# Row maxima of attention scores: reductions of up to 1024 columns over two PSUM banks, in a ring of two pairs, with one bank for the outputs

## The chip, the core and the metric

One Trainium2 chip, one of its cores. The metric is the device time of one execution in microseconds (us), as the median of several runs. TensorE (PE in the profile) multiplies, VectorE (DVE) and ScalarE (ACT) work on what it leaves in PSUM, GpSimd (POOL) does small work in SBUF, and SyncE (SP) issues most of the DMAs. PSUM has eight banks of 512 float32 values per partition. A matmul here writes into one bank at a time.

## The reference, cut to what matters

Two layers of a hybrid model run over 2048 tokens of width 128: a Mamba block, a mixture of experts, attention, experts again, a second Mamba block, a quantised MLP, attention with ALiBi, and the MLP again. The change touches the two attentions. Each has 16 heads of width 8, and is causal:

```python
dots = jnp.einsum('bhid,bhjd->bhij', q, k) * scale
causal = jnp.triu(jnp.ones((n, n), dtype=bool), k=1)
dots = jnp.where(causal, mask_value, dots)
attn = jax.nn.softmax(dots.astype(jnp.float32), axis=-1).astype(dots.dtype)
out = jnp.einsum('bhij,bhjd->bhid', attn, v)
```

The softmax subtracts each query's largest score before it exponentiates. That maximum is what the changed code finds.

## The kernel before

The 2048 tokens are NT = 16 tiles of 128 and NC = 4 chunks of 512. For each head, `attention` computes the scores twice.

The first time it does so with queries on the partitions, to find the maxima. An *item* is one query tile t against one key chunk kc, up to 512 keys wide; `q_items` lists the 40 items of a head, numbered 0 to 39 here. Tiles 0 to 3 have one item each (0 to 3), tiles 4 to 7 two each (4,5 to 10,11), tiles 8 to 11 three each (12,13,14 to 21,22,23) and tiles 12 to 15 four each (24..27 to 36..39). A tile's last item is 128, 256, 384 or 512 columns wide, in turn, and the others 512. PE makes an item with four matmuls of 32 weight columns each (L1679), which run side by side; DVE then takes its maximum, with `tensor_reduce` (L1861), or with `tensor_tensor_reduce` (L1858, CUSTOM_DVE in the profile, followed by a READ_ACCUMULATOR) where the item holds the diagonal and the causal mask must be added. After item 39, L1866 folds a tile's maxima together, GpSimd splits them into three bfloat16 parts (L1942 to L1947), PE transposes these (`turn`, L1663), DVE copies them out (L1849, CAST), and SP writes them by DMA into the operand `q_op` as three more rows (L2030).

The second time the scores come with keys on the partitions, the maxima already subtracted by those three rows. A *score* is a key tile against a query chunk (L1693, with a causal mask on the diagonal ones, L1697), 40 per head. ACT exponentiates it (L1797), and PE multiplies four at a time with v (`times_v`, L1715, float32, in two instructions each). When a query chunk is done, ACT copies the outputs from PSUM (L1805) and SP stores them.

PE's order is written out by hand: score b+3 of the running head, then the item at position 54+b of the item stream, and after every fourth b a `times_v`. So the items run one head and 14 positions ahead of the scores, and score 0 of a head comes right after item 10 of the next one. `times_v` stands behind items 1, 5, 9, 13 and so on; those behind items 13, 25 and 37 are diagonal ones with narrower pieces. The transposition `turn` of a head stands ahead of item TURN = 5 of the next. The first 54 items run before any score. Waits are in order on each engine.

PSUM: three banks `ps_k` for scores (KB = 3), three banks `ps_q` for items, transpositions and the later `direct` and `output` products (QB = 3), and two banks `ps_o` for the outputs. Each use of `ps_q` has a number, and `bank_free(use)` (L1650) lets PE write use u only when DVE has read use u-3. `times_v` waits at the start of a chunk only for the copy of the chunk before last (L1707), since two banks alternate.

```python
            def bank_free(use):
                if use >= QB:
                    pe.wait_ge(q_read, use - QB + 1)
```

Of the kernel before, what the change touches and what calls it, by code (L numbers as in the profile page):

```python
# [21 lines left out]
ALU = mybir.AluOpType  # L22
# [4 lines left out]
P = 128  # L27
# [1453 lines left out]
def attention(nc, g, w, tag, dram, x, xn, alibi):  # L1481
# [4 lines left out]
    with ExitStack() as ctx:  # L1486
# [6 lines left out]
        QB = 3  # L1493
        LEAD = 14
        TURN = 5
# [33 lines left out]
        maxes = m.sb("maxes", [P, NT, NC])  # L1529
# [58 lines left out]
        NQ = len(q_items)  # L1588
        q_begins = [min(i for i, (t, kc) in enumerate(q_items) if t // TPC == c) for c in range(NC)]
# [16 lines left out]
        item_use, turn_use = {}, {}  # L1606
        for p in range(POSITIONS):
            if turned_at(p) is not None:
                turn_use[turned_at(p)] = len(item_use) + len(turn_use)
            if p < NQ * HEADS:  # L1610
                item_use[p] = len(item_use) + len(turn_use)
        USES = len(item_use) + len(turn_use)
        direct_use = {(FULL, c): USES + 2 * c for c in range(NC)}
        output_use = {0: USES + 8, 1: USES + 9, 2: USES + 12, 3: USES + 13}
        direct_use.update({(LAST, 0): USES + 10, (LAST, 1): USES + 14, (LAST, 2): USES + 16, (LAST, 3): USES + 18})

# [20 lines left out]
        def _(pe):  # L1637
# [29 lines left out]
            def item(h, n):  # L1667
                t, kc = q_items[n]
                use = item_use[NQ * h + n]
                width = min(CH, (t + 1) * P - kc * CH)  # L1670
                if h == 0 and n in q_begins:
# [29 lines left out]
            def times_v(h, n):  # L1701

                c = k_items[n][0]
                if n == 0:
                    pe.wait_ge(v_ready, h + 1)
                if n in begins and NC * h + c >= 2:
                    pe.wait_ge(o_read, NC * h + c - 1)  # L1707
                pe.wait_ge(exp_done, NK * h + n + 4)
                for a, (r, lo, hi) in [(a, piece) for a in range(n, n + 4) for piece in pieces(a)]:
                    j, first = k_items[a][1:3]  # L1710
                    rows = slice(32 * r, 32 * r + 32)
                    if c == 0 and j:
                        pe.matmul(ps_o[rows, 0, 0:first], zeros[:, :], g["sel"][:, 0:j, :], start=True, stop=True,
                                  skip_group_check=True)
                    pe.matmul(ps_o[rows, c % 2, lo:hi], vh[h % SLOT][:, j, :], probs[:, a % PSLOT, lo - first:hi - first],  # L1715
                              start=j < 4, stop=j >= TPC * c, skip_group_check=True).then_inc(pv_done, 1)

            def direct(h, c):

                pe.wait_ge(o_read, NC * h + c + 1)  # L1720
                for i in range(2):
                    use = direct_use[h, c] + i
                    bank_free(use)
                    for j in range(2):
                        last = pe.matmul(ps_q[:, use % QB, j * DW:(j + 1) * DW], o_sb[:, c, tile(2 * i + j)],
                                         w_direct[:, h - FULL, :], start=True, stop=True)
                    last.then_inc(q_ready, 1)
# [56 lines left out]
        def _(act):  # L1784
# [14 lines left out]
            def output(h, c):  # L1799
                act.wait_ge(pv_done, h * PIECES + through[ends[c]])  # L1800
                if h == LAST:
                    act.wait_ge(q_ready, direct_use[FULL, c] + 2)
                elif h:
                    act.wait_ge(o_stored[c], h * STORES)
                act.activation(o_sb[:, c, :], ps_o[:, c % 2, :], ACT.Copy).then_inc(o_read, 1)  # L1805
# [22 lines left out]
        def _(dve):  # L1828
# [22 lines left out]
            def item(h, n):  # L1851
                t, kc = q_items[n]
                use = item_use[NQ * h + n]
                width = min(CH, (t + 1) * P - kc * CH)
                dve.wait_ge(q_ready, use + 1)
                found, bank = maxes[:, t, kc:kc + 1], ps_q[:, use % QB, 0:width]
                if kc == t // TPC:
                    dve.tensor_tensor_reduce(bank, bank, g["mask_q"][:, CH - width:CH], 1.0, -3e38, ALU.add, ALU.max,  # L1858
                                             found).then_inc(q_read, 1)
                else:  # L1860
                    dve.tensor_reduce(found, bank, AX.X, ALU.max).then_inc(q_read, 1)  # L1861
                if n == NQ - 1:
                    dve.wait_ge(q_read, use + 1)
                    if h:
                        dve.wait_ge(max_ready, h)
                    dve.tensor_reduce(neg_max[:, :], maxes[:, :, :], AX.X, ALU.max, negate=True).then_inc(neg_ready, 1)  # L1866
                    dve.wait_ge(neg_ready, h + 1)

            def add_direct(h, c):
                for i in range(2):  # L1870
                    use = direct_use[h, c] + i
                    bank = ps_q[:, use % QB, 0:2 * DW].rearrange("p (j f) -> p j f", f=DW)
                    dve.wait_ge(q_ready, use + 1)
                    dve.reciprocal(inv_col[:, i, :], bank[:, :, P]).then_inc(col_ready, 1)
                    if h == LAST:
                        dve.wait_ge(q_read, output_use[c] + 1)
# [4 lines left out]
                    last.then_inc(q_read, 1)  # L1881

            def add_output(c):
                use = output_use[c]
                dve.wait_ge(q_ready, use + 1)
                dve.wait_ge(q_read, direct_use[FULL, c] + 2)
                xc = x[:, TPC * c:TPC * (c + 1), :]
                dve.tensor_tensor(xc, ps_q[:, use % QB, :].rearrange("p (j f) -> p j f", f=P), xc, ALU.add).then_inc(q_read, 1)

            def norm_stats(c):  # L1890
                dve.wait_ge(q_read, direct_use[LAST, c] + 2)
                ahead.stats(dve, c)
# [266 lines left out]
def constants():  # L2159
# [11 lines left out]
    for s in range(SPL):  # L2171
# [14 lines left out]
        "c_mask_q": np.where(np.arange(CH)[None, :] - (CH - P) > k, NEG, 0.0).astype(np.float32),  # L2186
# [80 lines left out]
```

## Time and profile before

| | us |
|---|---|
| median of 3 runs | 1998.84 |
| lowest and highest run | 1994.96, 2001.33 |
| the profiled execution | 1991.66 |
| its span, first to last instruction | 1989.9 |
| mean granted TensorE clock | 0.965 of 2.4 GHz |

```profile
PE   6888888999799999999899978888888999999988
DVE  6899966666789999996556678999668999999855
PEclk9999998999789999999999998999996999999998
```

Each digit is a fortieth of the span, 49.7 us, and gives the busy share of that stretch in tenths (9 is 90% or more). The attentions are the two stretches in which PE and DVE are both at 9: from about 510 us to 950 us and from about 1480 us to 1930 us. The remaining rows stand in the section after the next.

### The profile page before, as it was taken

The page shows a single profiled execution, that of the slowest core. Times are in us where ns is not written, and L with a number is a line of the kernel's source. Part 1 is how long each engine was busy: PE and PEld are TensorE (multiplying, and loading weights), DVE is VectorE, ACT ScalarE, POOL GpSimd, SP SyncE. Part 2 cuts the span into 40 slices and gives each one's busy share as a digit, 9 for nine tenths or more (in the row PEclk, how much of TensorE's full clock was granted, in tenths as well). Part 3 has the DMA queues.
Part 4 walks back from the last instruction along what each step waited for, and adds up shares of the span by engine and source line. Part 5 has one row for each costly group of instructions (what it writes and reads, how often), then busy time and mean ns, then how long its engine had stood idle before and what let it go on. Part 6 is the DMA issues. An engine that isn't in the chain of part 4 may idle for free. (4 is left out here: it accounts for less than half of the span.)

```text
span 1989.9 us, 48041 instructions
## 1 busy us (share of the span) xinstructions
PE 1802.1 (91%) x18610; PEld 961.7 (48%) x18610; DVE 1585.1 (80%) x3424; ACT 1176.7 (59%) x2363; POOL 592.4 (30%) x556
## 2 busy tenths in 40 slices
PE   6888888999799999999899978888888999999988
PEld 2444454444355555555444434444543555555544
DVE  6899966666789999996556678999668999999855
ACT  4676623222268888887422257766352888888855
POOL 3899931000200000004000038999430000000142
PEclk9999998999789999999999998999996999999998
DMA  5433400311312222222041113343012222232200
GB/s 160 121 129 127 128 11 0 86 49 37 106 30 51 51 51 51 51 40 40 1 86 48 37 56 116 133 125 124 1 42 83 49 55 55 56 55 55 31 23 22
DMA packets 68801, 127.94 MB, mean 64 GB/s; under 512 B 20343, under 2 KB 30853, under 8 KB 67165
## 3 DMA queue, kind: packets, MB, share of 16 engines
q1 hardware_dynamic: 68284, 124.34, 24.3%
q8 instruction: 147, 2.41, 0.5%
q14 instruction: 82, 0.66, 0.1%
q10 hardware_dynamic: 288, 0.52, 0.1%
HBM read 107.15 MB, written 16.48 MB: 62 GB/s over the span
## 5 line engine op out<-in xcount | busy, mean ns | idle before, releaser
L1797 ACT ACTIVATE a_probs<-a_ps_k 128x512 f32<-128x512 f32 (+3 forms) x1280 | 599.6, 545 | 216.5 <-PE a_ps_k L1697 135.2
L1861 DVE TENSOR_REDUCE a_maxes<-a_ps_q 128x1 f32<-128x512 f32 x768 | 504.1, 685 | 66.9 <-PE a_ps_q L1679 64.2
L1679 PE MATMUL a_ps_q<-a_k_op,a_q_op 84*32 84x512 bf16 (+7 forms) x5120 | 536.3, 366 | 23.2 <-DMA a_k_op<-a_k_parts 8.7
L1693 PE MATMUL a_ps_k<-a_q_op,a_k_op 87*32 87x512 bf16 (+7 forms) x5120 | 513.0, 351 | 4.0 <-ACT a_probs L1797 3.4
L1715 PE MATMUL a_ps_o<-a_probs,a_vh 128*32 128x512 f32 (+3 forms) x2752 | 316.1, 505 | 0.8 <-ACT a_probs L1797 0.8
L1679 PEld LDWEIGHTS a_ps_q<-a_k_op,a_q_op 72*32 72x32 bf16 (+1 forms) x5120 | 187.1, 97 | 169.7 <-DVE a_maxes L1861 68.8
L1858 DVE CUSTOM_DVE_ANT_0 a_ps_q<-a_ps_q,all_c_mask_q 128x128 f32<-128x128 f32 (+3 forms) x512 | 248.1, 495 | 4.0 <-PE a_ps_q L1679 3.0
L1693 PEld LDWEIGHTS a_ps_k<-a_q_op,a_k_op 75*32 75x32 bf16 (+1 forms) x5120 | 184.1, 96 | 131.7 <-ACT a_probs L1797 78.6
L1113 ACT ACTIVATE e_silu<-e_psg,all_me_b 128x512 f32<-128x512 f32 x128 | 87.7, 687 | 228.1 <-PE e_psg L1045 228.1
L1942 POOL CAST a_max_parts<-a_neg_max 128x16 bf16<-128x16 f32 x32 | 6.3, 196 | 705.3 <-DVE a_neg_max L1866 705.3
L1196 DVE SCALAR_TENSOR_TENSOR e_mid<-e_psv,all_me_b,e_silu 128x512 f32<-128x512 f32 x128 | 95.6, 748 | 129.1 <-PE e_psv L1047 125.2
L172 POOL TENSOR_TENSOR all_rstd<-all_var_eps,all_c_minus_half 128x4 f32<-128x4 f32 x36 | 36.8, 1022 | 467.0 <-DVE all_var_eps L161 466.9
L668 POOL TENSOR_TENSOR m1st_read<-m1st_state,m1st_c_rows 128x1024 f32<-128x1024 f32 x64 | 149.6, 2358 | 11.2 <-PE m1st_psy L420 7.9
L596 DVE TENSOR_TENSOR_SCAN m1st_state<-m1st_decay,m1st_carry,m1st_drive 128x1024 f32<-128x1024 f32 x64 | 146.8, 2334 | 7.6 <-DVE m1st_drive L576 6.4
L668 POOL TENSOR_TENSOR m0st_read<-m0st_state,m0st_c_rows 128x1024 f32<-128x1024 f32 x64 | 149.6, 2359 | 10.7 <-DVE m0st_state L596 6.4
L596 DVE TENSOR_TENSOR_SCAN m0st_state<-m0st_decay,m0st_carry,m0st_drive 128x1024 f32<-128x1024 f32 x64 | 146.8, 2334 | 7.6 <-DVE m0st_drive L576 6.4
L1697 PE MATMUL a_ps_k<-all_c_mask_k,all_c_ident_b 128*32 128x128 bf16 x2048 | 148.5, 221 | 1.1 <-issue 0.9
L1045 PE MATMUL e_psg<-e_xT,all_me_w_T 128*128 128x512 f32 x256 | 133.9, 605 | 1.5 <-ACT e_xT L197 1.5
L1047 PE MATMUL e_psv<-e_xT,all_me_w_T 128*128 128x512 f32 x256 | 132.3, 599 | 0.0
L1034 PE MATMUL e_pso<-e_hid,all_me_w_T 128*128 128x512 f32 x256 | 119.6, 596 | 4.5 <-DVE e_hid L1205 4.5
L1715 PEld LDWEIGHTS a_ps_o<-a_probs,a_vh 128*32 128x32 f32 x2752 | 106.7, 110 | 26.2 <-ACT a_probs L1797 1.1
L420 PE MATMUL m1st_psy<-m1st_read,all_c_ident 128*128 128x512 f32 x256 | 116.1, 594 | 2.0 <-POOL m1st_read L668 1.8
(294 smaller groups left out, 2585.2 us busy)
## 6 DMA issues: line engine op xcount, KB each, us to landing
m0st_c_rows<-m_bc_rows SPq DMA_DIRECT2D x32, 512.0 KB
e_w_rows<-e_comb SPq DMA_DIRECT2D x64, 256.0 KB, 3.3
m1st_c_rows<-m_bc_rows SPq DMA_DIRECT2D x32, 512.0 KB
a_q_op<-a_q_parts SPq DMA_DIRECT2D x30, 288.0 KB
a_k_op<-a_k_parts SPq DMA_DIRECT2D x30, 288.0 KB
m0st_b_rows<-m_bc_rows SPq DMA_DIRECT2D x32, 256.0 KB
m1st_b_rows<-m_bc_rows SPq DMA_DIRECT2D x32, 256.0 KB
a_outputs<-a_o_sb SPq DMA_DIRECT2D x448, 18.0 KB
```

The lines of the kernel that those rows point to most:

```text
L596: dve.tensor_tensor_scan(state[half(q, h)][:, :], decay[half(q, h)][:, :], drive[:, h, :], carry[:, h, q % NS:q % NS + 1], ALU.mult, ALU.a ...
L668: pool.tensor_tensor(read[h][:, :], state[half(q, h)][:, :], c_rows[q % 2][:, :], ALU.mult).then_inc(read_ready, 1)
L1034: pe.matmul(pso[:, :], w["w3_T"][:, e, f, :], hid[:, k % SL, :], start=k == 0, stop=k == K - 1, skip_group_check=True).then_inc(hid_free, 1)
L1045: pe.matmul(psg[:, f, :], w["w1_T"][:, e, fs], xT[:, tokens(c)], start=True, stop=True).then_inc(g_ready, 1)
L1047: pe.matmul(psv[:, f, :], w["w2_T"][:, e, fs], xT[:, tokens(c)], start=True, stop=True).then_inc(v_ready, 1)
L1679: last = pe.matmul(ps_q[32 * r:32 * r + 32, use % QB, 0:width], q_op[h % SLOT][0:NR, part(t, r)], k_op[h % SLOT][0:NR, kc * CH:kc * CH + w ...
L1693: last = pe.matmul(ps_k[32 * r:32 * r + 32, b % KB, 0:width], k_op[h % SLOT][:, part(j, r)], q_op[h % SLOT][:, c * CH + first:c * CH + fir ...
L1697: last = pe.matmul(ps_k[32 * r:32 * r + 32, b % KB, 0:P], g["ident_b"][:, part(0, r)], g["mask_k"][:, :], start=False, stop=True, skip_gro ...
L1715: pe.matmul(ps_o[rows, c % 2, lo:hi], vh[h % SLOT][:, j, :], probs[:, a % PSLOT, lo - first:hi - first], start=j < 4, stop=j >= TPC * c, s ...
L1797: act.activation(probs[:, n % PSLOT, 0:width], ps_k[:, b % KB, 0:width], ACT.Exp).then_inc(exp_done, 1)
L1858: dve.tensor_tensor_reduce(bank, bank, g["mask_q"][:, CH - width:CH], 1.0, -3e38, ALU.add, ALU.max, found).then_inc(q_read, 1)
L1861: dve.tensor_reduce(found, bank, AX.X, ALU.max).then_inc(q_read, 1)
```

## The change

Two or one neighbouring items of a tile become a *find*: key chunks 0 and 1, and chunks 2 and 3. A find has one use of `ps_q`, which is now two slots of two banks each (QB = 2, 1024 columns a slot). PE writes a find's items side by side and signals only after the last; DVE takes the maximum of the whole find in one instruction, of up to 1024 columns. A head has 24 finds: items 0, 1, 2, 3 alone, (4,5), (6,7), (8,9), (10,11), then (12,13), 14, (15,16), 17, (18,19), 20, (21,22), 23, then (24,25), (26,27) and so on to (38,39). `bank_free` is asked once per find and now means that DVE has read the find before last. `turn` moves to the place ahead of item 6, where a find begins. The fourth pair's two banks come from `ps_o`, which shrinks to one bank: `times_v` waits at each chunk's start for the copy of the chunk just before. `direct` uses one slot instead of two banks. The mask is 1024 columns wide.

```diff
-        QB = 3
+        QB = 2
-        TURN = 5
+        TURN = 6
-        maxes = m.sb("maxes", [P, NT, NC])
+        maxes = m.sb("maxes", [P, NT, 2])
-        ps_q = m.ps("ps_q", [P, QB, CH])
+        ps_q = m.ps("ps_q", [P, QB, 2 * CH])
-        ps_o = m.ps("ps_o", [P, 2, CH])
+        ps_o = m.ps("ps_o", [P, CH])
+        finds = [(t, tuple(kc for kc in range(t // TPC + 1) if kc // 2 == half)) for t in range(NT) for half in range(t // TPC // 2 + 1)]
...
             def item(h, n):
-                bank_free(use)
+                if n == find_begins[f]:
+                    bank_free(use)
                 for r in range(4):
-                    last = pe.matmul(ps_q[32 * r:32 * r + 32, use % QB, 0:width], q_op[h % SLOT][0:NR, part(t, r)],
+                    last = pe.matmul(ps_q[32 * r:32 * r + 32, use % QB, at:at + width], q_op[h % SLOT][0:NR, part(t, r)],
-                last.then_inc(q_ready, 1)
+                if n == find_ends[f]:
+                    last.then_inc(q_ready, 1)
...
             def times_v(h, n):
-                if n in begins and NC * h + c >= 2:
-                    pe.wait_ge(o_read, NC * h + c - 1)
+                if n in begins and NC * h + c:
+                    pe.wait_ge(o_read, NC * h + c)
...
             def direct(h, c):
+                use = direct_use[h, c]
+                bank_free(use)
                 for i in range(2):
-                    use = direct_use[h, c] + i
-                    bank_free(use)
...
-                last.then_inc(q_ready, 1)
...
             def item(h, n):
+                if n != find_ends[f]:
+                    return
-                found, bank = maxes[:, t, kc:kc + 1], ps_q[:, use % QB, 0:width]
-                if kc == t // TPC:
-                    dve.tensor_tensor_reduce(bank, bank, g["mask_q"][:, CH - width:CH], 1.0, -3e38, ALU.add, ALU.max,
+                found, bank = maxes[:, t, kcs[0] // 2:kcs[0] // 2 + 1], ps_q[:, use % QB, 0:width]
+                if t // TPC in kcs:
+                    dve.tensor_tensor_reduce(bank, bank, g["mask_q"][:, 2 * CH - width:2 * CH], 1.0, -3e38, ALU.add, ALU.max,
```

## Rows read from the trace of the kernel before

**Rows 1.** Stretches; busy us of PE, PEld, DVE, ACT, POOL; clock, DMA share, GB/s.
```profile
588.00:612.40 24.40, 24.17 (x482) 14.22 (x477) 22.45 (x59) 20.21 (x46) 1.04 (x5) 1.00 0.26 42
...
100.00:150.00 50.00, 42.73 (x155) 21.65 (x154) 48.19 (x26) 35.62 (x78) 49.98 (x26) 1.00 0.36 127
...
950.00:1000.00 50.00, 43.16 (x228) 23.10 (x227) 28.45 (x109) 22.94 (x37) 3.05 (x3) 0.93 0.01 2
```
**Rows 2.** Waits of PE, whole span: us in total, times, longest.
```profile
PE m0st_drive L407 <- DVE m0st_state L596: 28.1, 30, 1.3
```
**Rows 3.** Waits of PE from 588 to 900 us, the only such row.
```profile
PE a_ps_q L1679 <- DVE a_maxes L1858: 3.0, 13, 0.2
```
**Rows 4.** Groups by shape, DVE: busy us, mean ns, idle time before.
```profile
L1861 DVE TENSOR_REDUCE a_maxes<-a_ps_q 128x1 f32<-128x512 f32 x768 | 504.1, 685 | 66.9 <-PE a_ps_q L1679 64.2
...
L576 DVE TENSOR_TENSOR m0st_drive<-m_du,m0st_drive 128x1024 f32<-128x1024 f32 x32 | 38.6, 1207 | 1.7 <-PE m0st_drive L396 1.7
```
**Rows 5.** Timeline of DVE: start, duration, line, tiles, shapes, count.
```profile
725.84 0.27 DVE L1849 CAST a_max_T<-a_ps_q 48x128 bf16<-48x128 f32 x1
...
729.98 0.69 DVE L1858 CUSTOM_DVE_ANT_0 a_ps_q<-a_ps_q,all_c_mask_q 128x512 f32<-128x512 f32 x1
730.59 0.14 DVE L1858 DVE_READ_ACCUMULATOR2_ANT a_maxes<- 128x1 f32 x1
730.59 1.28 DVE L1861 TENSOR_REDUCE a_maxes<-a_ps_q 128x1 f32<-128x512 f32 x2
...
750.24 0.27 DVE L1849 CAST a_max_T<-a_ps_q 48x128 bf16<-48x128 f32 x1
```
**Rows 6.** Head's boundary: items 39, 1, 2, 4, turn, item 5; SP's DMA.
```profile
746.14 0.41 PE L1679 MATMUL a_ps_q<-a_k_op,a_q_op 72*32 72x512 bf16 x4
...
746.90 0.29 PE L1679 MATMUL a_ps_q<-a_k_op,a_q_op 72*32 72x256 bf16 x4
...
748.10 0.36 PE L1679 MATMUL a_ps_q<-a_k_op,a_q_op 72*32 72x384 bf16 x4
...
748.92 0.41 PE L1679 MATMUL a_ps_q<-a_k_op,a_q_op 72*32 72x512 bf16 x4
...
749.36 0.24 PE L1663 MATMUL a_ps_q<-all_c_ident_b,a_max_parts 128*32 128x128 bf16 x2
749.83 0.24 PE L1679 MATMUL a_ps_q<-a_k_op,a_q_op 72*32 72x128 bf16 x4 [0.23 <-DVE a_maxes L1858]
...
750.53 0.77 SPq L2030 DMA_DIRECT2D a_q_op<-a_max_T  x1
```
**Rows 7.** The same timeline: a reduction of DVE that follows item 38.
```profile
746.15 0.69 DVE L1861 TENSOR_REDUCE a_maxes<-a_ps_q 128x1 f32<-128x512 f32 x1
```
**Rows 8.** Timeline of PE: score 0, then items 11 and 15.
```profile
729.15 0.39 PE L1693 MATMUL a_ps_k<-a_q_op,a_k_op 75*32 75x512 bf16 x4
...
729.43 0.39 PE L1679 MATMUL a_ps_q<-a_k_op,a_q_op 72*32 72x512 bf16 x4
...
731.37 0.54 PE L1679 MATMUL a_ps_q<-a_k_op,a_q_op 72*32 72x512 bf16 x4
```
**Rows 9.** Timeline of PE: items 22 and 24.
```profile
735.98 0.39 PE L1679 MATMUL a_ps_q<-a_k_op,a_q_op 72*32 72x512 bf16 x3
...
736.85 0.45 PE L1679 MATMUL a_ps_q<-a_k_op,a_q_op 72*32 72x512 bf16 x4
```
**Rows 10.** DMA issues: KB each, us from issue to landing.
```profile
a_inverses<-a1ou_inv SPq DMA_DIRECT2D x1, 112.0 KB, 2.0
```
**Rows 11.** Timeline: two of ACT's copies of the outputs, each with the next `times_v`.
```profile
734.30 0.59 ACT L1805 ACTIVATE a_o_sb<-a_ps_o 128x512 f32<-128x512 f32 x1
...
735.00 1.09 PE L1715 MATMUL a_ps_o<-a_probs,a_vh 128*32 128x512 f32 x8
...
746.43 0.59 ACT L1805 ACTIVATE a_o_sb<-a_ps_o 128x512 f32<-128x512 f32 x1
...
747.02 1.06 PE L1715 MATMUL a_ps_o<-a_probs,a_vh 128*32 128x512 f32 x8
```

More of the change, by code:

```diff
@@ L1588, in attention @@
         NQ = len(q_items)
+        finds = [(t, tuple(kc for kc in range(t // TPC + 1) if kc // 2 == half)) for t in range(NT) for half in range(t // TPC // 2 + 1)]
+        find_of = [f for f, (t, kcs) in enumerate(finds) for kc in kcs]
+        find_begins = [find_of.index(f) for f in range(len(finds))]
+        find_ends = [b - 1 for b in find_begins[1:]] + [NQ - 1]
         q_begins = [min(i for i, (t, kc) in enumerate(q_items) if t // TPC == c) for c in range(NC)]
@@ L1604, in turned_at @@
             return p // NQ - 1 if p >= NQ and p % NQ == TURN else None
-        item_use, turn_use = {}, {}
+        assert TURN in find_begins
+        find_use, turn_use = {}, {}
         for p in range(POSITIONS):
             if turned_at(p) is not None:
[L1609 to L1615, printed above, removed]
+                turn_use[turned_at(p)] = len(find_use) + len(turn_use)
+            if p < NQ * HEADS and p % NQ in find_begins:
+                find_use[p // NQ, find_of[p % NQ]] = len(find_use) + len(turn_use)
+        USES = len(find_use) + len(turn_use)
+        direct_use = {(FULL, c): USES + c for c in range(NC)}
+        output_use = {0: USES + 4, 1: USES + 5, 2: USES + 7, 3: USES + 8}
+        direct_use.update({(LAST, 0): USES + 6, (LAST, 1): USES + 9, (LAST, 2): USES + 10, (LAST, 3): USES + 11})
         def stream(turn, item, first, last):
@@ L1668, in item @@
                 t, kc = q_items[n]
-                use = item_use[NQ * h + n]
+                f = find_of[n]
+                use = find_use[h, f]
                 width = min(CH, (t + 1) * P - kc * CH)
+                at = kc % 2 * CH
                 if h == 0 and n in q_begins:
@@ L1712, in times_v @@
                     if c == 0 and j:
-                        pe.matmul(ps_o[rows, 0, 0:first], zeros[:, :], g["sel"][:, 0:j, :], start=True, stop=True,
+                        pe.matmul(ps_o[rows, 0:first], zeros[:, :], g["sel"][:, 0:j, :], start=True, stop=True,
                                   skip_group_check=True)
-                    pe.matmul(ps_o[rows, c % 2, lo:hi], vh[h % SLOT][:, j, :], probs[:, a % PSLOT, lo - first:hi - first],
+                    pe.matmul(ps_o[rows, lo:hi], vh[h % SLOT][:, j, :], probs[:, a % PSLOT, lo - first:hi - first],
                               start=j < 4, stop=j >= TPC * c, skip_group_check=True).then_inc(pv_done, 1)
@@ L1720, in direct @@
                 pe.wait_ge(o_read, NC * h + c + 1)
+                use = direct_use[h, c]
+                bank_free(use)
                 for i in range(2):
-                    use = direct_use[h, c] + i
-                    bank_free(use)
                     for j in range(2):
-                        last = pe.matmul(ps_q[:, use % QB, j * DW:(j + 1) * DW], o_sb[:, c, tile(2 * i + j)],
+                        last = pe.matmul(ps_q[:, use % QB, i * CH + j * DW:i * CH + (j + 1) * DW], o_sb[:, c, tile(2 * i + j)],
                                          w_direct[:, h - FULL, :], start=True, stop=True)
-                    last.then_inc(q_ready, 1)
+                last.then_inc(q_ready, 1)
             def output(c):
@@ L1869, in add_direct @@
             def add_direct(h, c):
+                use = direct_use[h, c]
+                dve.wait_ge(q_ready, use + 1)
+                dve.wait_ge(q_read, use)
                 for i in range(2):
-                    use = direct_use[h, c] + i
-                    bank = ps_q[:, use % QB, 0:2 * DW].rearrange("p (j f) -> p j f", f=DW)
-                    dve.wait_ge(q_ready, use + 1)
+                    bank = ps_q[:, use % QB, i * CH:i * CH + 2 * DW].rearrange("p (j f) -> p j f", f=DW)
                     dve.reciprocal(inv_col[:, i, :], bank[:, :, P]).then_inc(col_ready, 1)
-                    if h == LAST:
-                        dve.wait_ge(q_read, output_use[c] + 1)
+                if h == LAST:
+                    dve.wait_ge(q_read, output_use[c] + 1)
+                for i in range(2):
+                    bank = ps_q[:, use % QB, i * CH:i * CH + 2 * DW].rearrange("p (j f) -> p j f", f=DW)
                     dve.wait_ge(col_ready, use_number(h, c, i) + 1)
@@ L1880, in add_direct @@
                         last = dve.scalar_tensor_tensor(xt, bank[:, j, 0:P], inv_col[:, i, j:j + 1], xt, ALU.mult, ALU.add)
-                    last.then_inc(q_read, 1)
+                last.then_inc(q_read, 1)
             def add_output(c):
@@ L1885, in add_output @@
                 dve.wait_ge(q_ready, use + 1)
-                dve.wait_ge(q_read, direct_use[FULL, c] + 2)
+                dve.wait_ge(q_read, direct_use[FULL, c] + 1)
                 xc = x[:, TPC * c:TPC * (c + 1), :]
-                dve.tensor_tensor(xc, ps_q[:, use % QB, :].rearrange("p (j f) -> p j f", f=P), xc, ALU.add).then_inc(q_read, 1)
+                dve.tensor_tensor(xc, ps_q[:, use % QB, 0:CH].rearrange("p (j f) -> p j f", f=P), xc, ALU.add).then_inc(q_read, 1)
             def norm_stats(c):
-                dve.wait_ge(q_read, direct_use[LAST, c] + 2)
+                dve.wait_ge(q_read, direct_use[LAST, c] + 1)
                 ahead.stats(dve, c)
@@ L2185, in constants @@
         "c_minus_half": np.full((P, NT), -0.5, np.float32),
-        "c_mask_q": np.where(np.arange(CH)[None, :] - (CH - P) > k, NEG, 0.0).astype(np.float32),
+        "c_mask_q": np.where(np.arange(2 * CH)[None, :] - (2 * CH - P) > k, NEG, 0.0).astype(np.float32),
         "c_mask_k": np.where(k > q, NEG, 0.0).astype(bf),
```

11 lines of the change are left out of this document (6 added, 5 removed).

## The prediction

> **What bounds the kernel now.** I read the busy times by stretch first. In one head's period of the attention, 24.40 us, PE is busy for 24.17 us, DVE for 22.45 and ACT for 20.21 [rows 1]. So PE sets the pace and DVE, at 92%, is next. A busy PE need not be at its peak, so I looked at the waits: between 588 and 900 us the only idle time of PE with a releaser is 3.0 us in 13 pieces of 0.2, one per head, for a maximum of DVE [rows 3]. The timeline shows its place [rows 6]: item 5 starts at 749.83, 0.47 us behind the transposition at 749.36, which occupies PE for 0.06 us (128 columns). PE stood still for 0.41 us, because use u waits for the read of use u-3 and DVE was behind. Item 1 is late by another 0.05. That is **0.46 us per head**; elsewhere PE streams without a break. The period is the distance of two CASTs, 750.24 - 725.84 = 24.40 us [rows 5]. Hence whatever DVE saves can bring back at most 0.46 us per head, and each new wait of PE is added in full, since nothing else is late.
>
> **The durations.** DVE starts its next instruction before the last one's end. Two reductions of 512 take 1.28 together and 0.69 alone [rows 5, 7], so one costs 0.60 and its end is 0.09 later. A masked one of 512 costs 730.59 - 729.98 = 0.61, and its accumulator is read 0.14 beyond that [rows 5]. No 1024-column reduction exists yet. The nearest row is a `tensor_tensor` of 1024 from PSUM, 1207 ns against 685 for the reduction of 512 [rows 4]: 512 more columns are 0.52 to 0.53 us. I take **1.14 us** for a find of 1024, with or without mask, 1.0 to 1.3 for the range; a masked one of w columns is 0.08 us and w times 1.04 ns. DVE drops 16 of its 40 instructions per head and about 0.07 us with each: 1.2 us.
>
> On PE, two positions of score and item at full width take 736.85 - 735.98 = 0.87 us [rows 9], so one matmul group 0.22, in proportion for narrower ones, and a mask 0.06; `times_v` takes 0.86, a diagonal one 0.65. From the start of a 512-wide item to DVE's start are 0.38 + 0.06 = 0.44 us (0.39, 0.33, 0.28 for 384, 256, 128). The 0.06 is a semaphore: the reduction that ends at 746.84 lets item 1 start at 746.90 [rows 6, 7]. So PE may write a slot 0.09 + 0.06, about 0.14, after DVE's step with a plain reduction, and 0.14 + 0.06 = 0.20 after a masked one.
>
> **The new ring, find by find.** Two slots are four banks instead of three, but PE now waits for the find before last, and DVE can't begin a find until both its items are there. I go round a head once; "nominal" is PE's distance without a wait.
>
> Item 1 waits for find (38,39): item 39 + 0.44 + 1.14 + 0.20 = 1.78 us. Nominal is 0.76 in the trace, 0.05 of it waiting [rows 6], so 0.71: **stall 1.07**. Item 4 waits for item 2's read: 0.39 + 0.47 + 0.20 = 1.06, nominal 748.92 - 748.10 = 0.82 [rows 6]: **0.24**. Item 6 waits for find (4,5), 640 wide: 0.28 + 0.75 + 0.20 = 1.23 from item 5, nominal 0.06 + 0.86 + 0.22 + 0.06 = 1.20: **0.03**. Items 8 to 14 meet free slots (item 14: 1.78 after item 11, nominal 1.81).
>
> Item 15 waits for (12,13), which DVE reads after (10,11): item 11 + 0.44 + 1.14 + 1.14 + 0.14 = 2.86. Nominal runs from 729.43 to the last of the four matmuls that begin at 731.37, some 0.15 later [rows 8]: 2.09. **Stall 0.77**; the short find 14 lies between and fills a slot without giving DVE or PE time. Item 18 waits for (15,16): 0.44 + 1.14 + 0.14 = 1.72 from item 16, nominal 1.63 with a `times_v` in it: **0.09**. Item 21 waits for (18,19): 1.72 from item 19, nominal 0.22 + 0.06 + 0.16 + 0.16 + 0.06 + 0.11 = 0.78: **0.94**. Item 24 waits for (21,22): 1.72 from item 22, nominal 0.87 [rows 9]: **0.85**. From item 24 on all finds are two items long, four positions take PE 0.87 + 0.87 + 0.86 us and DVE at most 2.28, and no wait comes.
>
> So **1.34 at the start** of a head (items 1, 4, 6) and **2.65 in tiles 8 to 11** (items 15, 18, 21, 24).
>
> **The transposition, one place later.** It brings the maxima to score 0, which stands behind item 10. After it: 0.28 until the CAST, 0.27 for it, 0.03 until SP's DMA (now issued at 750.53 [rows 5, 6]), its landing, 0.06. Score 0 comes nominally 2.63 + 0.03 later (729.15 less item 6, a period before 750.97, and 0.06 for the transposition). The landing isn't shown for this DMA. Nothing waits for it now, 24.40 + 729.15 - 750.53 = 3.02 us after its issue, so it is under 2.96; the nearest small one landed in 2.0 [rows 10]. With 2.0 there is no stall, with 2.96 it is 0.94. I take 2.2, near the landing that a row shows: **0.18 us**. The queue of SP is free there: the four stores ahead are issued by about 748.4. GpSimd's chain isn't late: its maxima would come 0.36 us later, and the transposition over 2 us later.
>
> **One bank for the outputs.** The first `times_v` of a chunk now waits for the copy just before it. In the trace the copy starting at 746.43 ends at 747.02, exactly where `times_v` starts [rows 11]; that one is chunk 3's first, behind item 1, and is covered by that item's new stall of 1.07. The others leave more: the copy from 734.30 ends 0.11 us ahead of the `times_v` at 735.00, against the 0.06 of the semaphore. So 0; at worst a few hundredths for each of the others, 0.1 per head. Below nothing it can't go, since it only adds waits.
>
> **The sum.** Tiles 8 to 11 pass in 15 heads beside the scores, the start in 14 (the first 54 items run alone): 15 x 2.65 + 14 x (1.34 + 0.18 - 0.46) = 39.8 + 14.8 = 54.6 us per attention. In the lead-in DVE alone sets the pace. It saves 21 instructions, 1.5 us, but is left without work behind each short find, since PE fills a slot at 1.2 GHz there in 0.86 us: 1.04 + 0.91 + 0.78 + 0.64 = 3.4. That is +1.9. The ends (`direct` with one signal instead of two) I put at 0.3. Together 56.8, for two attentions **+113 us**. The profiled execution would go from 1991.66 to 2105. The median of before lies 0.36% above it; against the median I add the same sum: 1998.84 + 113 = **2112 us**, 5.7% slower.
>
> Of the bounds, 0.1 us on the 1024-column step moves items 1, 15, 21 and 24 by one step each, two for item 15, so 0.5 us per head and 15 us in all; 1.0 to 1.3 gives -21 to +24. The landing gives -5 to +21, the outputs up to +3. This case alone: 2085 to 2150.
>
> **A rule against the change.** PE stands still in small pieces while DVE works one long instruction. The Trainium skill, Perfetto Trace Analysis, section Optimizing Scalar/DVE Operations, says both that larger operations improve throughput if the engine is saturated, and that where an engine isn't saturated but causes bubbles on others, breaking instructions up may let work end sooner. With its figure of about 125 ns per PSUM access, 16 instructions less would be an estimated 2.0 us per head for DVE; the rows give 1.2. By its first half the kernel would gain, by its second it loses; rows 1 and 3 (PE at its limit, DVE not) put this case under the second.
>
> **The rivals.**
> 1. *DVE's load is what counts, faster.* Place: the start of each head, where DVE lags. If PE found a slot free each time, the 0.46 us would go: 2 x 14 x 0.46 = 13 us, 1986 us. It decides from the point at which item 21's slot is read 0.78 us after item 19, so if the step of 1024 took under 0.20 us. For it: DVE at 92%. Against it: 512 columns already take 0.60 us. 4%.
> 2. *Hidden or nearly so,* a balance of the two within 0.3%: would need stalls of 0.46 us per head in all. 3%.
> 3. *A cheaper long reduction,* 0.88 us, as if the second bank went at half the price: items 1, 15, 21 and 24 give back 0.26 each, item 15 another 0.26, item 18 all of its 0.09: 1.4 us per head, 41 us, 2071 us. Against it: 1207 ns for a 1024-column operation from PSUM [rows 4]. 10%.
> 4. *The clock falls too.* PE's busy share drops from 99% to some 86%. In the stretch after the attention the mean granted clock was 0.93 with PE busy for 43.2 of 50 us [rows 1]. A mean of 0.93 is 14% of the time at 1.2 instead of 2.4 GHz, 7% of the 23.9 us of streaming, 1.7 us per head or 50 us: 2162 us. Against it: in the Mamba stretch PE is busy for 42.7 of 50 with waits of up to 1.3 us at a clock of 1.00 [rows 1, 2]. 8%. The Trainium skill, TensorE: Matmul & The Clock Gate, section A second HAM failure mode: psum-queue depth-cycling, describes such an oscillation from frequent small pauses between groups; the Mamba rows speak against it here.
>
> **How the numbers follow.** My forecast has 75%. The range reaches down to rival 3 with some room, and up to 2152: 2060 to 2152. It leaves out rivals 1, 2 and 4. About 0.3% (6 us) is what a measurement can tell from no change: faster 0.04, same 0.03, slower 0.93.
>
> **What would show it.** The CASTs some 28 us apart instead of 24.40; PE idle in front of items 1, 15, 21 and 24, released by DVE's maxima, by 0.8 to 1.1 us each before the pipeline's tail; a reduction of 1024 with a mean of about 1.22 us; DVE's busy share per period falling to about three quarters; no idle time in tiles 12 to 15; the other stages unchanged. I am wrong if the long reduction is much shorter, if score 0 waits longer for its DMA, or if the `times_v` at chunk starts show waits for the copy.

## The result, and the profile after

The changed kernel takes 2116.47 us, the median of 4 runs from 2111.93 to 2117.58, beside 1996.90 us for the kernel before in the same rounds. The ratio of the runs is **1.0587 [1.0563, 1.0610]**, and the medians lie 119.6 us apart. The forecast was 2112. The profiled execution took 2116.43 us, 124.8 more than that of before (1991.66).

The page of the changed kernel: span, busy time with share, the three rows in fortieths of the span (52.9 us each).

```profile
span 2114.6 us, 47539 instructions
...
PE 1830.3 (87%) x18610; PEld 915.7 (43%) x18610; DVE 1580.9 (75%) x2912; ACT 1189.5 (56%) x2363; POOL 593.4 (28%) x556
...
PE   6888879998788888889899978888868888888987
DVE  7999875666777877775555579998577778777745
PEclk9999999999699999999999989999978999999999
```

PE and DVE, both at 9 in the attentions before, are at 8 and 7 now. Neither is saturated. They wait for each other.

One head of the first attention between two CASTs, 28.19 us apart; busy us of PE, PEld, DVE, ACT, POOL; clock, DMA share, GB/s. It answers to the first of [rows 1].

```profile
645.09:673.28 28.19, 25.15 (x479) 12.65 (x475) 22.30 (x43) 20.66 (x45) 1.04 (x5) 1.00 0.23 45
```

DVE issues 16 instructions less, yet is busy for only 0.15 us less than in [rows 1], and the period is 3.8 us longer at a granted clock of 1.00. Waits of PE between 640 and 920 us (total, times, longest) show for whom it waits:

```profile
PE a_ps_q L1687 <- DVE a_maxes L1873: 20.5, 30, 0.8
PE a_ps_q L1687 <- DVE a_maxes L1870: 9.0, 10, 0.9
PEld a_ps_k L1702 <- DMA a_q_op<-a_max_T: 3.5, 10, 0.4
PEld a_ps_o L1724 <- ACT a_o_sb L1814: 3.2, 10, 0.3
```

Ten heads, and in place of [rows 3]: three waits per head behind a plain reduction, one behind a masked one, one for the DMA that brings the maxima to score 0, and one for the copy of the outputs. The last two are waits of the weight load (PEld), which runs beside the matmuls, so PE itself loses less by them than they show. The two reductions by shape (busy us, mean ns, idle time before):

```profile
L1873 DVE TENSOR_REDUCE a_maxes<-a_ps_q 128x1 f32<-128x1024 f32 x256 | 313.1, 1223 | 94.8 <-PE a_ps_q L1687 94.6
L1870 DVE CUSTOM_DVE_ANT_0 a_ps_q<-a_ps_q,all_c_mask_q 128x1024 f32<-128x1024 f32 x64 | 78.9, 1233 | 21.7 <-PE a_ps_q L1687 21.5
```

In front of the long reductions DVE itself stands idle for 94.8 us, waiting for PE to fill the slot. PE waits for a slot of two banks to be read whole, then DVE waits for it to be filled whole. The timeline of one head has every such place. First tiles 8 to 11: start, duration, engine, line, operation, tiles, count, and in brackets the idle time before it with what released it. Rows between these are left out.

```profile
760.75 0.39 PE L1687 MATMUL a_ps_q<-a_k_op,a_q_op 72*32 72x512 bf16 x4
761.20 1.23 DVE L1870 CUSTOM_DVE_ANT_0 a_ps_q<-a_ps_q,all_c_mask_q 128x1024 f32<-128x1024 f32 x1 [0.65 <-PE a_ps_q L1687]
762.35 1.22 DVE L1873 TENSOR_REDUCE a_maxes<-a_ps_q 128x1 f32<-128x1024 f32 x1
763.48 0.29 DVE L1870 CUSTOM_DVE_ANT_0 a_ps_q<-a_ps_q,all_c_mask_q 128x128 f32<-128x128 f32 x1
763.62 0.40 PE L1687 MATMUL a_ps_q<-a_k_op,a_q_op 72*32 72x512 bf16 x4 [0.60 <-DVE a_maxes L1873]
766.29 0.39 PE L1687 MATMUL a_ps_q<-a_k_op,a_q_op 72*32 72x512 bf16 x4
766.73 1.22 DVE L1873 TENSOR_REDUCE a_maxes<-a_ps_q 128x1 f32<-128x1024 f32 x1 [0.60 <-PE a_ps_q L1687]
767.88 0.56 DVE L1870 CUSTOM_DVE_ANT_0 a_ps_q<-a_ps_q,all_c_mask_q 128x384 f32<-128x384 f32 x1
768.01 0.40 PE L1687 MATMUL a_ps_q<-a_k_op,a_q_op 72*32 72x512 bf16 x4 [0.77 <-DVE a_maxes L1873]
769.22 0.39 PE L1687 MATMUL a_ps_q<-a_k_op,a_q_op 72*32 72x512 bf16 x4
770.94 0.40 PE L1687 MATMUL a_ps_q<-a_k_op,a_q_op 72*32 72x512 bf16 x4 [0.68 <-DVE a_maxes L1873]
```

The PE rows are items 11, 15, 19, 21, 22 and 24. Item 19 starts at 766.29 and fills its slot; DVE begins at 766.73 and its step ends at 767.88; item 21 starts at 768.01, though item 20 between them took PE only a moment. The distance of 1.72 us is 0.44 of filling, 1.15 of reading and 0.13 of handing back. Items 22 to 24 repeat it, and items 11 to 15 hold it with two long steps (2.87).

The same view at the head's start: item 39, DVE's last find, item 1, the transposition, SP's DMA, and score 0, again without the rows between.

```profile
780.12 0.40 PE L1687 MATMUL a_ps_q<-a_k_op,a_q_op 72*32 72x512 bf16 x3
780.57 1.23 DVE L1870 CUSTOM_DVE_ANT_0 a_ps_q<-a_ps_q,all_c_mask_q 128x1024 f32<-128x1024 f32 x1 [0.16 <-PE a_ps_q L1687]
781.91 0.29 PE L1687 MATMUL a_ps_q<-a_k_op,a_q_op 72*32 72x256 bf16 x4 [0.90 <-DVE a_maxes L1870]
785.77 0.22 PE L1668 MATMUL a_ps_q<-all_c_ident_b,a_max_parts 128*32 128x128 bf16 x2
786.35 0.77 SPq L2045 DMA_DIRECT2D a_q_op<-a_max_T  x1
788.60 0.10 PEld L1702 LDWEIGHTS a_ps_k<-a_q_op,a_k_op 75*32 75x32 bf16 x4 [0.31 <-DMA a_q_op<-a_max_T]
```

Item 1 comes 1.79 us after item 39 (0.76 in [rows 6]). Between the transposition's DMA and score 0 lie 2.25 us, so with 0.06 for the semaphore it landed in 2.19.

### The profile page after: what moved, and what is told of

Same layout as the page of the kernel before. It is cut to its first block and busy times, and to the rows that moved or that the text cites. A ratio compares the mean times of both kernels' runs of the same rounds, so it can differ in the third digit from the quotient of the medians.

```text
span 2114.6 us, 47539 instructions
## 1 busy us (share of the span) xinstructions
PE 1830.3 (87%) x18610; PEld 915.7 (43%) x18610; DVE 1580.9 (75%) x2912; ACT 1189.5 (56%) x2363; POOL 593.4 (28%) x556
## 5 line engine op out<-in xcount | busy, mean ns | idle before, releaser
L1806 ACT ACTIVATE a_probs<-a_ps_k 128x512 f32<-128x512 f32 (+3 forms) x1280 | 611.8, 538 | 325.9 <-PE a_ps_k L1706 206.2
L1687 PE MATMUL a_ps_q<-a_k_op,a_q_op 84*32 84x512 bf16 (+7 forms) x5120 | 502.1, 369 | 117.7 <-DVE a_maxes L1873 72.2
L1702 PE MATMUL a_ps_k<-a_q_op,a_k_op 87*32 87x512 bf16 (+7 forms) x5120 | 502.0, 352 | 4.1 <-ACT a_probs L1806 2.3
L1870 DVE CUSTOM_DVE_ANT_0 a_ps_q<-a_ps_q,all_c_mask_q 128x128 f32<-128x128 f32 (+7 forms) x512 | 386.0, 769 | 94.0 <-PE a_ps_q L1687 84.6
L1873 DVE TENSOR_REDUCE a_maxes<-a_ps_q 128x1 f32<-128x1024 f32 x256 | 313.1, 1223 | 94.8 <-PE a_ps_q L1687 94.6
L1687 PEld LDWEIGHTS a_ps_q<-a_k_op,a_q_op 72*32 72x32 bf16 (+1 forms) x5120 | 151.6, 98 | 307.9 <-DVE a_maxes L1873 126.5
L1702 PEld LDWEIGHTS a_ps_k<-a_q_op,a_k_op 75*32 75x32 bf16 (+1 forms) x5120 | 166.5, 96 | 124.2 <-ACT a_probs L1806 63.6
L1706 PE MATMUL a_ps_k<-all_c_mask_k,all_c_ident_b 128*32 128x128 bf16 x2048 | 129.3, 222 | 0.0
L1724 PEld LDWEIGHTS a_ps_o<-a_probs,a_vh 128*32 128x32 f32 x2752 | 98.2, 110 | 53.0 <-ACT a_o_sb L1814 12.6
```

The costliest lines, as they stand in the source:

```text
L1687: last = pe.matmul(ps_q[32 * r:32 * r + 32, use % QB, at:at + width], q_op[h % SLOT][0:NR, part(t, r)], k_op[h % SLOT][0:NR, kc * CH:kc * ...
L1702: last = pe.matmul(ps_k[32 * r:32 * r + 32, b % KB, 0:width], k_op[h % SLOT][:, part(j, r)], q_op[h % SLOT][:, c * CH + first:c * CH + fir ...
L1706: last = pe.matmul(ps_k[32 * r:32 * r + 32, b % KB, 0:P], g["ident_b"][:, part(0, r)], g["mask_k"][:, :], start=False, stop=True, skip_gro ...
L1724: pe.matmul(ps_o[rows, lo:hi], vh[h % SLOT][:, j, :], probs[:, a % PSLOT, lo - first:hi - first], start=j < 4, stop=j >= TPC * c, skip_gro ...
L1806: act.activation(probs[:, n % PSLOT, 0:width], ps_k[:, b % KB, 0:width], ACT.Exp).then_inc(exp_done, 1)
L1870: dve.tensor_tensor_reduce(bank, bank, g["mask_q"][:, 2 * CH - width:2 * CH], 1.0, -3e38, ALU.add, ALU.max, found).then_inc(q_read, 1)
```

## Experiments

Besides the theory of the prediction (the depth of the ring, counted in finds, makes PE wait; the length of the reduction sizes each wait), the rivals were that the single output bank costs, that the later transposition costs, that the reduction itself is dear whatever the ring, and, in the second half, that the clock makes the lead-in longer.

**The output bank alone.** The kernel before with one bank `ps_o`.

```diff
-        ps_o = m.ps("ps_o", [P, 2, CH])
+        ps_o = m.ps("ps_o", [P, CH])
-                if n in begins and NC * h + c >= 2:
-                    pe.wait_ge(o_read, NC * h + c - 1)
+                if n in begins and NC * h + c:
+                    pe.wait_ge(o_read, NC * h + c)
```

> The kernel before with one bank for the outputs and nothing else changed: the chunk's first times_v waits for the copy just before it. Theory (the ring of two slots carries the whole loss): the copies end 0.11 us or more ahead of times_v in three of four chunks, and exactly with it in the fourth, so at most 0.06 us per head in that one place, partly hidden by the 0.05 that item 1 waits anyway: 0 to +2 us, a period of 24.40 to 24.46 us. Rival (the single output bank costs a good part of the 119 us): PE waits for the copy at each chunk's start, 0.3 us or more per chunk, at least 30 us in all.

Measured: 2001.68 us beside 1998.50, ratio 1.0017 [1.0002, 1.0031], so between 0.4 and 6 us; periods of 24.46 to 24.48 us against 24.40. The bank alone costs some 0.07 us per head, which is a small part of 119.6.

**The freed bank as a fourth single one.** As above, with four slots of one bank for `ps_q`, and one reduction per item.

```diff
-        QB = 3
+        QB = 4
```

> The kernel before with the same eight banks as the changed one (three, four, one), but the four banks of the ring used one item at a time, with reductions of 512. Theory: item 5 waits for item 2's read instead of item 3's, so the 0.41 us at the head's start goes, and item 1's 0.05; 0.06 may come for the copy in front of chunk 3's times_v. Period 23.95 to 24.05 us instead of 24.40, 28 periods: 10 to 13 us faster than before, about 1985 us. Rival (the loss is in the bank layout or in the outputs' single bank, whatever the ring holds): slower than before.

Measured: 1987.25 us beside 1998.50, ratio **0.9938 [0.9919, 0.9958]**, so 8 to 16 us faster than the kernel before: the fastest kernel of this study. One head between its CASTs, columns as above:

```profile
640.00:664.01 24.01, 24.01 (x481) 15.66 (x475) 22.49 (x59) 20.19 (x45) 1.03 (x5) 1.00 0.29 55
```

PE is busy without a gap, and item 1 is 0.71 us behind item 39. The same eight banks and the same number of columns give 24.01 us as four slots and 28.2 as two. DVE has its 16 more instructions here and is busy for 22.49 us, and none of that is late. It follows that the way in which the banks are cut into slots decides, and neither the banks themselves nor DVE's load. Two slots instead of four and one long reduction instead of two short ones are still one change here; the next run parts them.

**Two reductions per find, same ring.** The changed kernel, in which DVE reads the first item of a two-item slot as soon as it is there and the slot is given back after the second.

```diff
                 if n == find_ends[f]:
                     last.then_inc(q_ready, 1)
+                else:
+                    last.then_inc(q_half, 1)
...
                 if n != find_ends[f]:
+                    dve.wait_ge(q_half, h * (NQ - len(finds)) + n - f + 1)
+                    dve.tensor_reduce(found, bank, AX.X, ALU.max)
                     return
```

> The changed kernel, but DVE reads a find of two items with two reductions of up to 512, the first as soon as the first item is there; the slot is still given back only after the second. Same two slots. Theory (PE waits for the slot's release, which comes late because the long reduction begins only after the second item): the stalls shrink to about 0.70 (item 1), 0.24 (item 4), 0 (item 6), 0.30 (item 15), 0 (item 18), 0.50 (item 21), 0.31 (item 24), 2.05 us per head instead of 4.0, and 0.15 for the DMA stays: period about 26.1 us, in all about 2057 us. Rival (the number of slots alone counts, however they are read): a period of 28.2 us, 2116 us, or more, since DVE has 16 instructions more.

Measured: 2052.89 us, ratio 1.0276 [1.0254, 1.0298], some 63 us less than the changed kernel, period 26.27. The distances shrink from 1.78 to 1.41 (items 39 to 1), from 2.87 to 2.40 (11 to 15) and from 1.72 to 1.30 and 1.19 (19 to 21, 22 to 24). Waits of PE between 640 and 900 us:

```profile
PE a_ps_q L1688 <- DVE a_maxes L1876: 5.3, 10, 0.5
PE a_ps_q L1688 <- DVE a_maxes L1879: 3.5, 10, 0.4
```

These are ten heads again. Thirty waits behind plain reductions, 20.5 us together, have become ten, 3.5 us together (L1879), and those behind masked ones (L1876) have gone from 9.0 to 5.3. The slot still comes back only after all of its columns are read. So about half of the loss comes from DVE beginning only when the slot's last item is in. This is what the Trainium skill, Perfetto Trace Analysis, section Optimizing Scalar/DVE Operations, says of breaking instructions up where they cause bubbles on other engines; the trace agrees, by 63 us. The other half stays with the two slots: with reductions of 512 and one output bank in both kernels, four slots take 1987 us and two take 2053.

**A reduction that costs half.** The changed kernel, with plain reductions that read only the first 512 of their 1024 columns.

```diff
-                    dve.tensor_reduce(found, bank, AX.X, ALU.max).then_inc(q_read, 1)
+                    dve.tensor_reduce(found, ps_q[:, use % QB, 0:CH], AX.X, ALU.max).then_inc(q_read, 1)
```

> The changed kernel with the plain reductions of a find of 1024 reading its first 512 columns only (8 per head; the masked ones stay), so that part of the maxima is left out. Slots, signals and PE's work are the same. Theory: each plain find gives its slot back 0.54 us sooner; the distance from item 11 to 15 becomes 2.32 us instead of 2.86, 19 to 21 and 22 to 24 1.18 instead of 1.72, 16 to 18 its nominal 1.62; item 1, whose find is masked, keeps 1.78. 1.7 us less per head, a period of 26.5 us, 51 us less than the changed kernel, about 2065 us. Rival (DVE's load is not what PE waits for, the two slots' signals are): 28.2 us as before.

Measured: 2061.05 us, ratio 1.0328 [1.0295, 1.0362]; period 26.50. Its waits of PE between 640 and 900 us:

```profile
PE a_ps_q L1687 <- DVE a_maxes L1870: 9.0, 10, 0.9
PE a_ps_q L1687 <- DVE a_maxes L1873: 2.5, 10, 0.3
```

The waits behind the masked reduction, untouched, are 9.0 us as in the changed kernel; the thirty behind plain ones have become ten, 2.5 us together. Items 39 to 1 keep 1.78, 11 to 15 lose 0.53, 19 to 21 and 22 to 24 come to 1.20 and 1.19. Each stall therefore contains the reduction's own length, once or twice, as the sum had it. DVE's busy time per head fell by 4.1 us and the period by 1.7: only the steps that a slot waits for count.

**Short finds last.** The changed kernel, tiles 8 to 11 with their four pairs first and their four single items after them.

```diff
+        finds.sort(key=lambda f: (f[0] // TPC, f[0] // TPC == 2 and f[1][0] == 2))
+        q_items = [(t, kc) for t, kcs in finds for kc in kcs]
```

> The changed kernel with another order in tiles 8 to 11: their four pairs of items first, then their four single items, instead of pair, single, pair, single. Same instructions, same slots, same reductions. Theory (what costs in tiles 8 to 11 is a single item between two pairs, which takes a slot but gives DVE no time): stalls there of about 0.17 (item 16), 1.05 (item 21) and 0.25 (item 24), 1.46 us instead of 2.65, a period of 27.0 us, 35 us less than the changed kernel, about 2081 us. Rival (what costs is the long reduction as such, wherever it stands): no change, 2116 us.

Measured: 2075.43 us, ratio 1.0383 [1.0363, 1.0404]; period 27.02, as forecast. So 41 us of the loss came from the order alone: a one-item find between two pairs takes one of the two slots and gives neither engine time. The shorter period is 35 of them; another 2.2 and 1.9 lie in the two lead-ins, which this order shortens too.

**The transposition later, in a ring without stalls.** The kernel with four single banks, and TURN = 8.

```diff
-        TURN = 5
+        TURN = 8
```

> The ring of four single banks with one output bank, and the transposition of the maxima ahead of item 8 instead of item 5. It measures the path of the maxima to score 0 by itself, without ring waits. Theory: from the transposition to score 0 are needed 0.28 + 0.27 + 0.03 + a DMA of 2.2 + 0.06 = 2.84 us; PE's nominal distance there is 1.81, so score 0 waits 1.0 us for the DMA in each of 14 or 15 heads: a period of 25.0 us instead of 24.01, 29 us in all, about 2016 us. Rival (the DMA lands well within the distance, and the place of the transposition costs nothing): 24.0 us, 1987 us.

Measured: 2025.28 us, ratio 1.0149 [1.0111, 1.0187]; period 25.37, 1.36 above the same kernel with TURN = 5. Its timeline, from the transposition to score 0:

```profile
705.49 0.22 PE L1663 MATMUL a_ps_q<-all_c_ident_b,a_max_parts 128*32 128x128 bf16 x2
706.04 0.28 DVE L1849 CAST a_max_T<-a_ps_q 48x128 bf16<-48x128 f32 x1
706.35 0.77 SPq L2030 DMA_DIRECT2D a_q_op<-a_max_T  x1
708.67 0.40 PE L1693 MATMUL a_ps_k<-a_q_op,a_k_op 75*32 75x512 bf16 x4 [1.21 <-DMA a_q_op<-a_max_T]
```

Score 0 stands behind a chain that does not shrink: 0.55 to the CAST (I had expected 0.28; DVE was in an item), 0.31 to the DMA, and 2.32 until score 0, so a landing of 2.26. The later transposition is a true cost; the change moved it by one item only, and its own wait is small.

**Filling PE in the lead-in.** The lead-in is the stretch from the first item of an attention to its first score. From about its start the granted clock was 0.50, for 37.5 and 34.1 us before the change and for 44.4 in both attentions after it, and the lead-ins had grown by more than forecast. Would a busier PE have a higher clock and shorten them? First the kernel with four banks and a bfloat16 matmul of 512 columns behind each item of the lead-in, then the changed kernel with the same.

```diff
-            stream(turn, item, 0, NQ + LEAD)
+            for p in range(NQ + LEAD):
+                stream(turn, item, p, p + 1)
+                pe.matmul(ps_o[:, :], g["ident_b"][0:SPL * 2 * NS, :], g["sel"][:, 0:TPC, :], start=True, stop=True,
+                          skip_group_check=True)
```

> The ring of four single banks with one output bank, and, in the lead-in (the 54 items that run before the first score), one extra bfloat16 matmul of 512 columns into the idle output bank behind each item. It asks what the half clock of the lead-in (about 35 us at 1.2 GHz from the first item on) costs. Theory: DVE sets the pace of the lead-in, 0.6 us an item, so the extra matmuls cost nothing once the clock has risen; if it rises well ahead of item 54, the 10 us of PE-bound work behind the last lead-in item that now run at 1.2 GHz run at 2.4: 3 to 5 us less per attention, 6 to 10 in all, about 1979 us. Rival (the granted clock does not rise for such filling, or the extra work delays the items): the same 1987 us or up to 10 us more.

> The changed kernel with the same extra matmuls in its lead-in. Theory: its lead-in is 5 us longer per attention than before's since a slot of two items takes PE 0.86 us to fill at 1.2 GHz, so that DVE runs dry in front of nearly every find; at 2.4 GHz it takes 0.44 and DVE runs dry in tiles 8 to 11 only. From item 4 to item 40 about 19 to 20 us instead of 23.2, and 2 us less behind it: about 6 us per attention, 12 in all, 2104 us. The period of the heads stays 28.2 us. Rival (the lead-in is longer for DVE's sake, whatever PE's clock): 2116 us or more.

Measured: 2036.63 us, ratio 1.0195 [1.0169, 1.0221], and 2153.30 us, ratio 1.0781 [1.0747, 1.0816]; both expectations of a gain missed, and the first run lies far above its rival's 10 us too. Two stretches of the first, one in the lead-in and one that ends 6.7 us behind the first score:

```profile
530.00:550.00 20.00, 18.93 (x95) 3.92 (x91) 11.50 (x28) 0.00 (x0) 0.00 (x0) 0.50 0.43 132
560.00:590.00 30.00, 30.00 (x207) 8.98 (x206) 17.29 (x43) 3.42 (x8) 1.04 (x5) 0.50 0.01 2
```

PE was busy for 18.9 of 20 us, then for 30 of 30, at 0.50 throughout. The clock was at half for 61.4 and 58.0 us in both kernels, and rose 6.4 us after the first score. Each added matmul only made the lead-in longer, 55.7 us instead of 30.5. Then the same with a float32 matmul of 128 columns, in both kernels.

```diff
-            stream(turn, item, 0, NQ + LEAD)
+            for p in range(NQ + LEAD):
+                stream(turn, item, p, p + 1)
+                pe.matmul(ps_o[:, 0:P], g["ident"][:, :], g["ident"][:, :], start=True, stop=True)
```

> The ring of four with, behind each of the 54 lead-in items, one extra float32 matmul of 128 columns instead of the bfloat16 one of 512. In the run with the latter the clock stayed at 1.2 GHz for 61 us though PE was busy for 95% of it, and rose 6 us after the first scores and times_v. Theory A (float32 matmuls over the whole array, as in times_v, bring the clock up): it rises within the first 10 us of the lead-in, and the lead-in takes DVE's 0.6 us an item: 1978 to 1985 us. Theory B (no filling brings it up as long as the items run alone): the half clock lasts to 6 us behind the first score, the item and the filling take 1.0 us at 1.2 GHz: about 15 us longer per attention, 2015 us.

> The changed kernel with the same float32 filling. If the clock rises in the lead-in, item 4 to item 40 takes 19 to 20 us instead of 23.2, since a slot is filled in 0.44 us and not 0.86, and what follows at half clock is shorter: about 2104 us, which would show that 4 us per attention of the changed kernel's loss lie in the half clock of the lead-in. If it doesn't, PE fills a slot in 1.7 us with the extra work and the kernel is slower than the changed one, 2125 us or more.

Measured: 2054.22 us, ratio 1.0283 [1.0256, 1.0311], and 2173.16 us, ratio 1.0885 [1.0863, 1.0906]. The lead-in of the first:

```profile
530.00:570.00 40.00, 38.90 (x196) 19.48 (x192) 20.54 (x43) 0.00 (x0) 0.00 (x0) 0.50 0.24 74
```

PE was busy for 38.9 of 40 us, and the clock was at 0.50 again. Theory B had the clock right but not the price: the lead-in grew by 35 us per attention and not by 15. No run had a whole lead-in at the full clock, so what the half clock costs there was not measured.

## Why the prediction was right

In the two profiled executions the 124.8 us lie so: from the first to the last score of each attention +54.6 and +55.2, the two lead-ins (first item to first score) +5.2 and +5.0, the ends -0.1 each, and +4.9 in stages that the change does not touch, among them the experts behind the first attention (from PE's first to its last matmul there 183.9 us before, 185.6 after) and the second Mamba block (262.7 and 265.2). These move by such amounts between kernels that differ in nothing there (the second Mamba block took 265.3 with one output bank and 263.0 with the ring of four), and the profiled execution of before lies below its own median; against the medians the whole is 119.6.

**The steady state** was forecast at 54.6 per attention and measured at 54.6 and 55.2, a period of 28.2 against about 28. The distances, as medians over the heads, each from the last of an item's four matmuls to the last of the other's:

| items | forecast, us | after | before |
|---|---|---|---|
| 39 to 1 | 1.78 | 1.78 | 0.75 |
| 2 to 4 | 1.06 | 1.06 | 0.82 |
| 4 to 5 | the wait of 0.41 gone | 0.45 | 0.88 |
| 5 to 6 | 1.23 | 1.23 | 1.15 |
| 11 to 15 | 2.86 | 2.87 | 2.09 |
| 16 to 18 | 1.72 | 1.72 | 1.61 |
| 19 to 21 | 1.72 | 1.72 | 0.78 |
| 22 to 24 | 1.72 | 1.72 | 0.87 |
| 24 to 39 | no wait | 9.19 | 9.23 |

They came out because each is a chain of steps that the trace of before already showed: fill, reduce, hand back. **The reduction of 1024** steps in 1.13 to 1.15 us (762.35 to 763.48, 761.20 to 762.35) against 1.14 taken, and its mean is 1.22. The runs with half reads (26.50 against 26.5 expected) and with split reads (26.27 against 26.1) confirm the mechanism, and the ring of four single banks shows that with slots enough the sixteen more reductions of a head cost PE no wait.

**The transposition:** landing 2.19 us against 2.2, wait of score 0 about 0.15 against 0.18. That this came out so well is in part luck. The one row near it was a DMA of another size with a landing of 2.0, by which there would have been no wait at all, and nothing on record gave the 0.2 that was added.

**The output bank** was put at 0, at worst 0.1 per head. Alone, in the kernel before, it costs 0.07 per head. Some 0.05 of it falls at chunk 3's first `times_v`, which stood exactly at the copy's end before and starts 0.05 us behind it with the single bank. In the changed kernel this `times_v` starts 1.04 us behind the copy, covered by item 1's stall, as the sum had it. The first `times_v` of chunk 2 starts 0.06 us behind the copy there (0.12 before), so the copy binds, which the sum did not see; the others leave 0.9 us and more. The distance from item 24 to 39, which holds this place, did not grow (9.19 against 9.23), so no cost of it can be read from the trace.

**The lead-in** is the term that was mis-sized: +1.9 forecast, +5.2 and +5.0 measured. DVE's idle time behind the short finds of tiles 8 to 11 was counted, and is there. But at the clock of 0.50 a pair takes PE 1.1 us from the handing back of its slot to DVE's start, which is longer than any masked reduction below 1024 columns. The timeline of DVE behind the last finds of tiles 11, 12 and 13:

```profile
544.45 1.23 DVE L1873 TENSOR_REDUCE a_maxes<-a_ps_q 128x1 f32<-128x1024 f32 x1 [0.57 <-PE a_ps_q L1687]
545.59 0.82 DVE L1870 CUSTOM_DVE_ANT_0 a_ps_q<-a_ps_q,all_c_mask_q 128x640 f32<-128x640 f32 x1
...
546.83 1.22 DVE L1873 TENSOR_REDUCE a_maxes<-a_ps_q 128x1 f32<-128x1024 f32 x1 [0.35 <-PE a_ps_q L1687]
...
549.20 1.23 DVE L1873 TENSOR_REDUCE a_maxes<-a_ps_q 128x1 f32<-128x1024 f32 x1 [0.22 <-PE a_ps_q L1687]
```

Only the first of these was in the sum. A masked find of 640 columns should step in 0.75 us and took 546.83 - 545.59 = 1.24; tiles 12 to 14 lose 0.49, 0.35 and 0.23, 1.1 us in all. Another 1.8 lies in places of the same kind: 0.31 and 0.24 beyond the step behind the last finds of tiles 5 and 7, and 0.23, 0.18 and 0.81 us of idle DVE in the first items of the second head (the last behind the transposition). That makes 2.9 of the missing 3.2 in the first attention, if the one idle piece of the kernel before, 0.27 us, is set against the 0.27 by which the first pair is read later. The sum treated DVE as the pace-maker wherever a find was long; at that clock PE and DVE take turns almost everywhere. The run with split reads bears this out: DVE has more instructions there, and still the lead-ins are shorter, 34.8 and 34.3 us instead of 36.5 and 36.3. The **ends** were put at +0.3 and measured at -0.1: `direct` with one slot costs nothing.

**The range.** The single bounds of the sum (24 for the reduction, 21 for the landing, 3 for the outputs) add up to 2160 us and not to the 2150 that the prediction gives for its own case. The result did not come near either.

**DVE's share** per period fell to 79%, not quite to three quarters. The forecast took 1.2 us of fewer steps off its busy time, but busy fell by only 0.15. Back to back, the last 0.09 us of a reduction lie under the next one and count once; now DVE stands idle before some 15 of its instructions per head instead of some 8, and each such end is counted.

**The rivals.** DVE's load as what counts: the ring of four gained about 11 us (medians), near the 13 of that rival, by giving PE its slots in time, with DVE's load unchanged. A cheaper long reduction: it takes 1223 ns, 538 more than the 685 of 512 columns, so the second bank comes at the full price. The clock: 1.00 in the heads with PE busy for 89% of the period and stalls of about 1 us. The oscillation that the Trainium skill describes under TensorE: Matmul & The Clock Gate, section A second HAM failure mode: psum-queue depth-cycling, did not come.

## What to carry to other kernels

Before you merge operations over several PSUM banks, count the slots of the ring and follow one through fill, read and hand-back: bigger operations save DVE 0.07 us each, but a ring of two turns every one of them into 0.44 + 1.15 + 0.13 us of alternation wherever the other engine has less than that to do in between. A bank that can be spared is worth more as one more slot of the old size: here about -11 us against +119.6 for the same eight banks. Look for short uses between long ones too; they occupy a slot and bring no time.

## What of the hardware was unexpected

The granted clock in the lead-in. In the kernel before, with items alone, PE was busy for 91% of a stretch of the lead-in; with bfloat16 or float32 matmuls between them for 95 to 100%. The clock stayed at 0.50 (1.2 GHz) for 34 to 72 us. In the profiles it rose 5 to 9 us after the first score and 1 to 5 us after the first `times_v`. In the first attention the first score, the first `times_v` and the rise were at 556.1, 560.2 and 563.2 us before the change, at 561.5, 565.6 and 569.8 after it, and at 592.9, 597.0 and 600.4 with the float32 filler. The Trainium skill, TensorE: Matmul & The Clock Gate, section The HAM clock gate (the "warmup" mystery), ties the clock to how busy PE has been; busy time as the profile counts it was not enough here. Whether it is the scores or the `times_v` that raise it stays open, as does whether a lead-in at the full clock would be shorter.
